# A two-layer graph kernel: the two row scalings change engines, POOL pauses at every third indirect transfer, and scatters wait for their turn once in four groups

## The reference

```
x   = layernorm(x + segment_max(relu(concat(x[dst], x[src]-x[dst]) @ W1 + b1) @ W2 + b2, dst))  # 0 where a row has no edge
agg = segment_sum(x[src], dst)
h   = relu((x + agg) @ V1 + c1) @ V2 + c2
out = layernorm(x + x @ Wres + bres + h)
```

## Time and profile before

| what | value |
|---|---|
| median of 3 timed runs | 1345.21 us (1344.24 to 1346.85) |
| the profiled execution | 1332.02 us, its span 1330.2 us |
| mean granted TensorE clock | 0.952 |
| busy: PE, DVE, ACT, POOL | 1123.7, 1068.6, 799.8, 825.8 us |
| share of the span | 84%, 80%, 60%, 62% |
| instructions | 32,137 |

### The profile page before, as it was taken

The page is one execution under the profiler, slowest core; times in us unless marked ns, Lnnn a source line. Parts: engine busy times, 40 slices in busy tenths (PEclk is TensorE's granted clock), DMA queues, the critical chain, the costliest instruction groups (busy, mean ns, idle before and its releaser), DMA issues. The chain is left out here.

```text
span 1330.2 us, 32137 instructions
## 1 busy us (share of the span) xinstructions
PE 1123.7 (84%) x7512; PEld 853.2 (64%) x7512; DVE 1068.6 (80%) x5491; ACT 799.8 (60%) x2305; POOL 825.8 (62%) x797
## 2 busy tenths in 40 slices
PE   2699999998888878788759999999999999999500
PEld 1577777765555545455448888888887777777400
DVE  6599999989887887898838999999987888888400
ACT  0366666666665656667526666666666777777400
POOL 5666666656666666666256666666665666655654
PEclk9899999999998999999979999999999999999855
DMA  4477777756665667666436565656564556656310
GB/s 111 141 220 214 214 220 212 222 188 195 183 208 180 199 174 210 177 205 196 141 112 191 187 185 186 185 187 187 189 190 140 177 181 190 185 181 200 103 38 28
DMA packets 160366, 233.86 MB, mean 176 GB/s; under 512 B 26815, under 2 KB 69273, under 8 KB 160284
## 3 DMA queue, kind: packets, MB, share of 16 engines
q1 hardware_dynamic: 133612, 193.69, 46.7%
q0 software_dynamic: 25088, 38.81, 11.0%
q10 hardware_dynamic: 1584, 0.53, 0.2%
HBM read 129.48 MB, written 90.12 MB: 165 GB/s over the span
## 5 line engine op out<-in xcount | busy, mean ns | idle before, releaser
L1277 PE MATMUL psY<-wcr,xT 128*128 128x128 f32 x1568 | 305.0, 276 | 0.0
L1276 PE MATMUL psY<-wc,hT 128*128 128x128 f32 x1568 | 304.6, 276 | 0.0
L586 POOL DMA_INDIRECT edge_rows<-x1e_table,idx x196 | 210.8, 1075 | 133.2 <-DMA edge_rows<-x1e_table,idx 77.6
L593 POOL DMA_INDIRECT out<-edge_rows,idx x196 | 202.2, 1031 | 129.5 <-issue 76.4
L586 POOL DMA_INDIRECT edge_rows<-in_x,idx x196 | 206.9, 1056 | 116.0 <-DMA edge_rows<-in_x,idx 67.3
L586 POOL DMA_INDIRECT xd_rows<-in_x,idx x196 | 203.5, 1038 | 115.9 <-DMA xd_rows<-in_x,idx 67.3
L1276 PEld LDWEIGHTS psY<-wc,hT 128*128 128x128 f32 x1568 | 255.8, 193 | 15.0 <-issue 8.3
L1123 ACT ACTIVATE o_rows<-psY,rs_b 128x128 f32<-128x128 f32 x784 | 223.0, 367 | 66.7 <-DVE rs_b L741 66.5
L1277 PEld LDWEIGHTS psY<-wcr,xT 128*128 128x128 f32 x1568 | 239.9, 193 | 0.0
L1287 PE MATMUL psH<-xT,wc 128*128 128x512 f32 x392 | 204.5, 604 | 16.0 <-DVE deltas L787 10.6
L1103 ACT ACTIVATE sd_a<-mv_a,eps_col 128x4 f32<-128x4 f32 x196 | 58.3, 298 | 239.6 <-DVE mv_a L677 239.6
(11 more groups left out here) (135 smaller groups left out, 2042.6 us busy)
## 6 DMA issues: line engine op xcount, KB each, us to landing
x_in<-in_x SPq DMA_DIRECT2D x196, 256.0 KB
out<-o_rows SPq DMA_DIRECT2D x196, 256.0 KB
xs_rows<-edge_rows SPq DMA_DIRECT2D x98, 256.0 KB, 2.9
xs_rows<-src_dram SPq DMA_DIRECT2D x49, 256.0 KB, 4.3
mask<-mask_dram SPq DMA_DIRECT2D x98, 128.0 KB, 3.6
x1e_table<-shared SPq DMA_DIRECT2D x49, 256.0 KB, 2.8
x1eT_spill<-x1eT SPq DMA_DIRECT2D x49, 256.0 KB
x1eT<-x1eT_spill SPq DMA_DIRECT2D x49, 256.0 KB, 2.8
```

The costliest lines, as they stand in the source:

```text
L586: nc.gpsimd.indirect_dma_start(to, None, table, bass.IndirectOffsetOnAxis(idx[:, what, t:t + 1], 0), bounds_check=rows - 1, oob_is_err=err ...
L593: nc.gpsimd.indirect_dma_start(table, bass.IndirectOffsetOnAxis(idx[:, SCAT, t:t + 1], 0), frm, None, bounds_check=N - 1, oob_is_err=False ...
L1276: t_.matmul(to[:, cut(t)], h[:, cut(t)], wc2[:, :], start=False, stop=False, skip_group_check=True)
L1277: last = t_.matmul(to[:, cut(t)], xt[:, cut(t)], wcr[:, :], start=False, stop=t == TILES - 1, skip_group_check=True)
```

## The change

There are four edits.

1. `norm1_scale` (x_in to x1) moves from DVE, where it was one instruction on 512 columns, to ACT, in four instructions of 128 columns. It stands where `finish` stood, behind the second root.
2. `finish` (psY to o_rows) moves from ACT to DVE, as one instruction on 512 columns. It stands at the end of the step, behind rs_b's reciprocal. In the steps of C and S the statistics of x_in are cut 1 + 3 tiles and not 2 + 2, and the three stand before that reciprocal. In A they are cut 2 + 2 over the even and the odd step.
3. POOL pauses at every third indirect transfer.
4. The wait for the stores comes once for a quad of groups, with the count of the quad's last group.

```
             def pace(kw):
                 issued[0] += 1
-                if issued[0] % 2 == 0:
+                if issued[0] % 3 == 0:
                     kw["engine_sem"] = s_issued
-            def issued_pair():
-                if issued[0] % 2 == 0:
-                    pool.wait_ge(s_issued, issued[0] // 2)
+            def issued_burst():
+                if issued[0] % 3 == 0:
+                    pool.wait_ge(s_issued, issued[0] // 3)
...
             def stores_needed(g):
-                earlier = pool.value_load(stores_16[0:1, g:g + 1], min_val=0, max_val=16 * LAST)
+                top = g + SLOTS - 1
+                earlier = pool.value_load(stores_16[0:1, top:top + 1], min_val=0, max_val=16 * LAST)
...
-                if g < WHOLE:
+                if g < WHOLE and r == 0:
                     for k in range(SLOTS):
                         pool.wait_ge(stored[k], count)
...
-                    if t == TILES - 1 and g + 1 < WHOLE:
+                    if t == TILES - 1 and r == SLOTS - 1 and g + 1 < WHOLE:
                         count = stores_needed(g + 1)
...
@@ vector @@
+            def finish(b, k):
+                b, k = unit(b, k)
+                if is_unit(b, k):
+                    dve.wait_ge(rstd2_done, b * SLOTS + k + 1)
+                    wait(dve, stored[k], 16 * b)
+                    scale(o_rows[:, k, :], psY[k % 2], rs_b[:, k, :], o_done)
             def dense(b, k):
                 norm1_ready(b, k + 2)
                 norm2_stats(b, k - 3)
                 norm1_var(b, k + 2)
                 norm2_ready(b, k - 3)
-                norm1_scale(b, k + 1)
+                norm1_stats(b, k + 3, range(0, 1))
                 norm2_var(b, k - 3)
                 norm1_recip(b, k + 2)
-                norm1_stats(b, k + 3, range(0, 2))
+                norm1_stats(b, k + 3, range(1, TILES))
                 norm2_recip(b, k - 3)
-                norm1_stats(b, k + 3, range(2, TILES))
+                finish(b, k - 3)
...
@@ scalar @@
+            def norm1_scale(b, k):
+                b, k = unit(b, k)
+                if is_unit(b, k):
+                    n = b * SLOTS + k
+                    act.wait_ge(rstd1_done, n + 1)
+                    wait(act, t_done, n - 1)
                     for t in range(TILES):
-                        last = a.activation(o_rows[:, k, cut(t)], psY[k % 2][:, cut(t)], ACT.Copy,
-                                            scale=rs_b[:, k, t:t + 1])
+                        last = a.activation(x1[:, k % 2, cut(t)], x_in[:, k, cut(t)], ACT.Copy,
+                                            scale=rs_a[:, k, t:t + 1])
...
             def second_half(b, k):
                 root2(b, k - 3)
-                finish(b, k - 3)
+                norm1_scale(b, k + 1)
```

More of the change, by code:

```diff
@@ L116, in gnn_program @@
         WHOLE = E // ROWS
+        assert WHOLE % SLOTS == 0
         last_dst = sb("last_dst", [1, WHOLE], I32)
@@ L587, in gather @@
                                              bounds_check=rows - 1, oob_is_err=err, **kw).then_inc(done, 16)
[L588 removed]
+                issued_burst()
             def scatter(table, frm, t, done):
@@ L594, in scatter @@
                                              bounds_check=N - 1, oob_is_err=False, **kw).then_inc(done, 16)
-                issued_pair()
+                issued_burst()
             def gather_src(g):
@@ L710, in norm1_recip @@
                     v.reciprocal(rs_a[:, k, :], sd_a[:, k, :]).then_inc(rstd1_done, 1)
[L712 to L718, removed]
             def norm2_stats(b, k):
@@ L796, in step_s @@
                 norm2_ready(b, r - 3)
-                norm1_scale(b, r + 1)
+                norm1_stats(b, r + 3, range(0, 1))
                 norm2_var(b, r - 3)
                 norm1_recip(b, r + 2)
-                norm1_stats(b, r + 3, range(0, 2))
+                norm1_stats(b, r + 3, range(1, TILES))
                 norm2_recip(b, r - 3)
-                norm1_stats(b, r + 3, range(2, TILES))
+                finish(b, r - 3)
                 keep_places(j, r - 3)
@@ L905, in step_a @@
                     norm1_var(b, k + 2)
-                    norm1_scale(b, k + 1)
+                    norm1_stats(b, k + 3, range(0, 2))
                 if b is not None and h % 2 == 1:
@@ L911, in step_a @@
                     norm2_var(b, k - 3)
-                    norm1_stats(b, k + 3)
+                    norm1_stats(b, k + 3, range(2, TILES))
                     norm2_recip(b, k - 3)
+                    finish(b, k - 3)
             def segment_sum(j, r):
@@ L980, in step_b @@
                 if b is not None:
-                    norm1_stats(b, r + 3)
+                    norm1_stats(b, r + 3, range(1, TILES))
+                    finish(b, r - 3)
             v.memset(eps_col[:, :], EPS)
@@ L1115, in root2 @@
                     root(sd_b[:, k, :], mv_b[:, k, :, :], std2_done)
-            def finish(b, k):
+            def norm1_scale(b, k):
                 b, k = unit(b, k)
                 if is_unit(b, k):
-                    act.wait_ge(rstd2_done, b * SLOTS + k + 1)
-                    wait(act, stored[k], 16 * b)
+                    n = b * SLOTS + k
+                    act.wait_ge(rstd1_done, n + 1)
+                    wait(act, t_done, n - 1)
                     for t in range(TILES):
-                        last = a.activation(o_rows[:, k, cut(t)], psY[k % 2][:, cut(t)], ACT.Copy,
-                                            scale=rs_b[:, k, t:t + 1])
-                    last.then_inc(o_done, 1)
+                        last = a.activation(x1[:, k % 2, cut(t)], x_in[:, k, cut(t)], ACT.Copy,
+                                            scale=rs_a[:, k, t:t + 1])
+                    last.then_inc(x1_done, 1)
             def first_half(b, k):
@@ L1231, in step_b @@
                 if b is not None:
-                    finish(b, r - 3)
+                    norm1_scale(b, r + 1)
                 finish1(j, r - 2)
@@ L1236, in _ @@
             root1(0, 1)
+            norm1_scale(0, 0)
             act.wait_ge(s_w, 16 * 11)
```

1 line of the change is left out of this document (removed).

## The result

| | before | after |
|---|---|---|
| median beside each other | 1346.03 us (1344.24 to 1347.82, 4 runs) | 1676.77 us (1669.30 to 1688.34, 4 runs) |
| ratio | | 1.2476, interval 1.2397 to 1.2556 |
| profiled execution, span | 1332.02, 1330.2 us | 1688.34, 1686.5 us |
| granted clock, mean | 0.952 | 0.903 |

The account below looks back on a forecast made before the run. POOL's queue was taken to bound the end, dense work next. POOL's run: 652.8 - 22 - 33 - 10 = 588 us; after a 30 us wait for stores, about 1300.5 profiled, plus 13: 1313 us, range 1290 to 1338.

Parts of the forecast that it names:

- S, A, B: Stages S, A and B: the swap of scalings costs S 4 us, A 0, B 0; POOL's run starts at 672.
- the third transfer does not follow freely: Rival in POOL's queue: a burst's third transfer idles 0.81 us or more, giving 1351 or 1386 us; chance 0.12.
- Step 1: POOL's transfers: without DVE's scalings with both operands in SBUF, their lengthening shrinks, 22 us off POOL's run.
- Step 2: POOL's pauses: 65 fewer at 0.51 us, 33 us off, if the third of a burst follows after 0.30.
- Step 3: POOL's turn, with its load of the count, comes 12 times and not 48: 10 us off.
- the gate for groups 44 to 47: POOL's scatters near the end: these groups start only when body 47 is stored, so the dense stage's end decides.
- one such wait, of 30 us: POOL before group 44: there at 1232, it waits 30 us for body 47's stores; first scatter at 1261.6.
- the last step of the sum: From profiled to timed: before's 13 us difference is added to about 1300.5, giving 1313 us.
- The swap in C: Dense stage C: the loop through DVE and ACT becomes 3.63 us a unit, not 3.44; 13 us lost.
- the slower side: Whole kernel slower than before: chance 0.11, of which 0.10 from the third transfer not following freely.

Follow-up runs that it names:

- third group: Kernels run on one chip beside the kernel before (1342.10 us); there, the two scalings swapped, pause at every second transfer, waits per group: 1354.95 us, ratio 1.0107.
- shorter unpaused tail: Kernel before with the turn once for four groups and, from transfer 753 on, a pause only at every 8th: 1332.18 us, ratio 0.9932.
- second group: Kernels with other pauses, on one chip beside the kernel before (1333.59 us); pause at every transfer: 1529.42 us with the swap of scalings, 1540.00 without.
- tail kernel: Kernel before, but POOL's last 48 transfers pause at every 8th and not every 2nd: 1323.84 us, ratio 0.9922.

## Why the prediction was wrong, point by point

**The step that failed** is in "S, A, B" and in the choice behind it: the prediction priced the bursts by POOL's own idle time ("33 us off, if the third of a burst follows the second after 0.30") and gave the dense stages nothing but the swap's price, S 4, A 0, B 0. They lost about 93, 50 and 226 us. No rival had it either: "the third transfer does not follow freely" looked for the price of a burst in POOL's queue, and it lies with those who wait for PE. Shown in its place: the burst alone, without the swap, costs 276 us (1637.85 against 1361.41), and the signals of PE's finished tiles rise up to 17.2 us late in that trace; one burst of 24 costs the dense work 22 us, and 24 memsets don't. Nothing in before's trace stood against it, but nothing priced it: no row had a third, and I asked only what a third costs its own engine.

**Step 1, POOL's lengthened transfers (22 us): nearly right.** The page after has means of 1010 ns and 996 against medians of 1000 and 984, where they were 78 and 49 apart:

```profile
L594 POOL DMA_INDIRECT out<-edge_rows,idx x196 | 195.2, 996 | 381.6 <-DMA out<-o_rows 187.4
...
L587 POOL DMA_INDIRECT edge_rows<-x1e_table,idx x196 | 197.9, 1010 | 135.6 <-issue 72.3
```

That is 196 x (0.068 + 0.037) = 21 us. The dense work was slow there, which could flatter it; with the swap on pairs at nearly full rate (third group) the scatters' mean is 987, the gathers' 1039. Before's trace shows it directly: of its scatters between 1020 and 1230 us the 62 that ran beside an x1 scaling took 0.156 us over the median on average, the other 60 nothing. So the scaling with both operands in SBUF was all of it in C, and about half in B.

**Step 2, the pauses: right for POOL.** The 196 gathers from the table took 292.8 us (807.8 to 1100.6); before's 321.2, less 13.3 of the shorter transfers and 16.7 of the pauses, is 291.2. The rival of the third transfer is refuted: in bursts of eight and of 24 each follows after 0.30. By the Trainium skill, "Advanced Engine Details and Errata", section "Engine Queue Depths", GPSIMD's queue has eight entries. No run here shows that depth: no burst of eight has a wait, which fits, but in the burst of 24 eighteen follow at 0.30 before 0.61 and 3.31 come, and what those two waited for no row tells.

**Step 3, the turn: its 10 us were never seen by themselves.** They can come only where POOL sets the end. Alone the turn brought nothing, with POOL waiting 7.2 us for the stores before group 44; with the shorter unpaused tail it came to 10 us in all, where 6 for the pauses and 10 for the turn were the terms. Its price, the gate for groups 44 to 47 on body 47's stores, decided as forecast, and two earlier quads as well. POOL, first transfer of quads 36, 40 and 44:

```profile
1414.99 0.98 POOL L594 DMA_INDIRECT out<-edge_rows,idx  x1 [94.59 <-DMA out<-o_rows]
...
1527.92 0.98 POOL L594 DMA_INDIRECT out<-edge_rows,idx  x1 [89.52 <-DMA out<-o_rows]
...
1648.34 0.98 POOL L594 DMA_INDIRECT out<-edge_rows,idx  x1 [97.38 <-issue]
```

The forecast had one such wait, of 30 us, ending at 1261.6. It ended at 1648.3, 387 us later, and from there 28.1 us to the last scatter's start at 1676.4, where 27.4 were forecast. So the whole miss is the dense work's lateness. One more difference lay in the last step of the sum: the 13 us between before's timed median and its profiled execution. That execution (1332.02) is like the undisturbed ones of the second group (1333.59), and the timed ones are not, so late signals may well be those 13 us; no trace of a timed execution shows it.

**The swap in C: right.** DVE in a stretch of C with POOL idle, against the loop of the earlier trace rows:

```profile
1500.21 0.18 DVE L736 RECIPROCAL rs_b<-sd_b 128x4 f32<-128x4 f32 x1 [0.50 <-ACT sd_b L1106]
1500.42 0.69 DVE L685 TENSOR_TENSOR o_rows<-psY,rs_b 128x512 f32<-128x512 f32 x1
1501.03 0.88 DVE L675 BATCH_NORM_STATS2 bn_b<-psY 128x6 f32<-128x128 f32 x4
...
1503.80 0.18 DVE L736 RECIPROCAL rs_b<-sd_b 128x4 f32<-128x4 f32 x1 [0.50 <-ACT sd_b L1106]
```

3.59 us a unit where 3.63 was forecast; the reciprocal to bn_b is 0.82 (0.85), and the wait for the root is still in every unit. Over the 64 units to the end of body 47 (bn_b of unit 191 less that of unit 127) the swap with a pause at every transfer takes 233.4 us, against 219.1 of the kernel before with the same pauses on the same chip: 14 where 13 was forecast. In S its price is hidden: with POOL idle a unit takes 4.5 us before and after. But with pairs the swap seems more exposed to late signals than the kernel before is: its ratio is 1.011 where that takes 1342 us and 1.052 where it takes 1361. Why it is more exposed wasn't tried: with the finish on DVE a late psY holds up statistics, root, reciprocal and output on one engine, and that is argued, not shown.

**The chances.** I gave the slower side 0.11, all but 0.01 of it for a mechanism that no run showed. What the range lacked was a case "the edit changes another engine's rate", for an edit that changes how often one engine's queue is allowed to rest.

## What to carry to other kernels

A pause in a queue that looks like plain idle time can be what others live on: before taking one out, try it in one place, with a burst of a few dozen transfers, and look at the others' waits there, on more than one chip. When waits have a releaser that the profile can't name, compare the start with the end of the work that made the tile; a lag of 0.03 us is prompt, one of 5 or 20 is a late signal and not late work. And pauses can be dropped where nobody works beside them, as in the last 48 transfers here, for 0.8%; with the last 32 and the turn for a quad it was 0.7%. Starting them while the dense work still had five units cost all of it.

Compare two kernels on one chip only. The pause at every transfer looked like a cure here because it ran on the one chip of the four whose traces show no late signal with pairs either.

## What the hardware showed that I had not expected

- PE's signals to DVE and ACT came up to 36 us late beside bursts of eight indirect transfers, 22 us late beside one of 24 and up to 17 us late beside threes. Those between DVE and ACT were within 0.1 us but for 17 in all the traces (1.8 us at most), and PE started within 0.05 us of ACT's xT in the middle of the burst of 24. Why it is PE's signals is open; no run separates the writing of descriptors from the DMAs that they start.
- With pairs it depends on the chip, or on something that changed with it, since each chip was used at one time only. The kernel before, as profiled, had no late signal, and neither had the traces of the second group, where it took 1334 us; on the chips where it took 1342, 1342 and 1361 us the traces with pairs have them, 5.0 to 8.7 us late at most, and the version that differs from it in the turn alone waits 80 us for them there. Threes with a wait for the landing still had late ones, up to 3.1 us, but only two "remote" waits, of 0.6 us in S and 1.8 in C. The last two units of the tail kernel, which met the first 5 us of a burst of eight, lost nothing, but on the chip without late signals: how much room, for how long, is not measured.
- PE loses twice: after it has idled for a late signal, its granted clock has fallen (a mean of 0.86 in S, 0.85 in B), and psH's two matmuls, 1.02 us before, take 2.08 after the 11.63 us of idle in the burst's trace, at a granted clock of 0.50: 1.2 GHz in place of 2.4.
